# Small triangular systems kept with the row outermost: strides moved from two transposes to the products and copies around them

## What is computed

```python
def step(S, inp):                       # for every mode m and head h
    q_t, k_t, v_t, b_g, b_beta = inp
    S = S * jnp.exp(b_g)[..., None, None]
    kv = jnp.einsum('mbhk,mbhkv->mbhv', k_t, S)
    dv = (v_t[None] - kv) * b_beta[..., None]
    S = S + k_t[..., :, None] * dv[..., None, :]
    o_t = jnp.einsum('mbhk,mbhkv->mbhv', q_t, S)
    return (S, o_t)
_, ys = jax.lax.scan(step, S0, (qt, kt, vt, gt, bt))
```

## Time and profile before

| | us |
|---|---|
| median of 3 runs | 6816.04 |
| lowest, highest | 6806.51, 6821.66 |
| profiled execution | 6782.06 |
| its span, first to last instruction | 6780.4 |
| VectorE busy | 5129.9 |
| PE busy | 4499.9 |
| ScalarE busy | 3431.5 |
| POOL busy | 2767.9 |

### The profile page before, as it was taken

The page is one execution under the profiler, slowest core; times in us unless marked ns, Lnnn a source line. Parts: engine busy times, 40 slices in busy tenths (PEclk is TensorE's granted clock), DMA queues, the critical chain, the costliest instruction groups (busy, mean ns, idle before and its releaser), DMA issues. The chain is left out here.

```text
span 6780.4 us, 195918 instructions
## 1 busy us (share of the span) xinstructions
PE 4499.9 (66%) x78513; PEld 3871.6 (57%) x78513; DVE 5129.9 (76%) x9800; ACT 3431.5 (51%) x6010; POOL 2767.9 (41%) x1789
## 2 busy tenths in 40 slices
PE   1666666667666666666667666676666666655993
PEld 1556655556655656655566555566555665553662
DVE  4888888888888888888888888888888888881003
ACT  1555555555555555555555555555555555542220
POOL 3444343444343444443444444443434444433003
PEclk6788888888878888888888878788788888877996
DMA  2000000000000000000000000000000000013123
GB/s 91 2 6 6 6 5 6 6 5 3 5 5 5 6 6 6 6 5 6 5 5 3 5 5 6 5 6 6 5 6 5 6 3 5 5 35 110 61 69 108
DMA packets 77480, 109.71 MB, mean 16 GB/s; under 512 B 20577, under 2 KB 66209, under 8 KB 75425
## 3 DMA queue, kind: packets, MB, share of 16 engines
q1 hardware_dynamic: 67616, 71.42, 3.3%
q0 software_dynamic: 8960, 25.39, 1.2%
HBM read 57.89 MB, written 38.89 MB: 14 GB/s over the span
## 5 line engine op out<-in xcount | busy, mean ns | idle before, releaser
L1573 POOL TENSOR_TENSOR state<-state,gc_end 128x512 f32<-128x512 f32 x512 | 592.2, 1174 | 1626.7 <-PE bank L595 1586.2
L572 PE MATMUL bank<-state,ke 128*64 128x64 f32 x16384 | 641.4, 246 | 310.2 <-DVE outT L1309 169.4
L572 PEld LDWEIGHTS bank<-state,ke 128*64 128x64 f32 x16384 | 607.9, 159 | 379.8 <-issue 189.7
L608 PE MATMUL last_two<-dvs,kte 128*64 128x64 f32 x16384 | 691.8, 248 | 180.3 <-DVE dvs L1298 180.2
L589 PE MATMUL bank<-rhs,te 128*64 128x64 f32 x8192 | 408.0, 252 | 521.4 <-DVE rhs L1291 284.5
L847 ACT ACTIVATE ke<-kq 32x512 f32<-32x512 f32 x1024 | 643.0, 628 | 201.4 <-DVE kq L1223 187.7
L1272 DVE TENSOR_TENSOR last_two<-last_two,prod 128x31 f32<-128x31 f32 (+15 forms) x1984 | 693.0, 349 | 68.1
L608 PEld LDWEIGHTS last_two<-dvs,kte 128*64 128x64 f32 x16384 | 629.5, 161 | 196.6 <-DVE dvs L1298 187.3
L1270 DVE TENSOR_TENSOR prod<-bd,last_two 128x31 f32<-128x31 f32 (+15 forms) x1984 | 670.4, 338 | 68.3
L797 ACT ACTIVATE te<-tt 32x256 f32<-32x256 f32 x1024 | 421.9, 412 | 565.1 <-DVE tt L1275 554.5
L589 PEld LDWEIGHTS bank<-rhs,te 128*64 128x64 f32 x8192 | 341.1, 161 | 599.3 <-DVE rhs L1291 550.6
(11 more groups left out here) (257 smaller groups left out, 10393.1 us busy)
## 6 DMA issues: line engine op xcount, KB each, us to landing
w_sb<-in_L_ffn_W_dram SPq DMA_DIRECT2D x16, 1024.0 KB, 9.4
expert_rows<-ke SPq DMA_DIRECT2D x1, 8192.0 KB, 21.9
xrows<-expert_rows SPq DMA_DIRECT2D x16, 512.0 KB, 8.5
expert_outputs<-yrow POOLq DMA_DIRECT2D x16, 512.0 KB, 3.4
xt<-_attn_hidden_states_dram SPq DMA_DIRECT2D x32, 128.0 KB, 2.8
xr<-_attn_hidden_states_dram SPq DMA_DIRECT2D x32, 128.0 KB, 2.1
x_after_attention<-xr SPq DMA_DIRECT2D x32, 128.0 KB, 1.7
xo<-x_after_attention SPq DMA_DIRECT2D x32, 128.0 KB, 3.7
```

Of the source, the lines that this page charges most:

```text
L572: mm = pe.matmul(bank_mem[g][s, q % 4 * DK:q % 4 * DK + DK], ke[:, c, r, q, s], state[:, hh * HQ + q, r, :], start=(r == 0), stop=(r == 1))
L608: mm = pe.matmul(bank_upd[g][s, (q % 4) * P + r * DK:(q % 4) * P + r * DK + DK], kte[:, r, q, s], dvs[:, q, :], start=True, stop=True)
L1573: pool.tensor_tensor(sv, sv, gc_end[:, vh, 4 * g:4 * g + 4, c].unsqueeze(2).broadcast_to([P, 4, 2 * DK]), ALU.mult).then_inc(sem(f"state_f ...
```

## The change

`at` and `tt` are kept with the row outermost and chunk and group innermost. Both transposes then have contiguous patterns on both sides. The products of `chunk_systems` write `at` with a step of 32 floats, and the copies of `expand_te` read `tt` with a step of 32 floats. The number of instructions, their order and all semaphores stay the same.

```diff
-        tt = sb("tt", [P, NC, HQ, C])
+        tt = sb("tt", [P, C, NC, HQ])
...
-        at = cos_t[:].rearrange("p q t -> p (q t)").rearrange("p (c q i) -> p c q i", c=NC, q=HQ)
+        at = cos_t[:].rearrange("p q t -> p (q t)").rearrange("p (i c q) -> p i c q", i=C, c=NC)
...
-                    ins = act.activation(te[s, :, 32 * m:32 * m + 32], tt[s, c, :, :], ACT.Copy)
+                    ins = act.activation(te[s, :, 32 * m:32 * m + 32], tt[s, :, c, :].rearrange("p i q -> p q i"), ACT.Copy)
...
-                ln(dve.tensor_tensor(at[:, c], bv[:, :, 0, :], bd[:, :, c, :], ALU.mult))
+                ln(dve.tensor_tensor(at[:, :, c, :].rearrange("p i q -> p q i"), bv[:, :, 0, :], bd[:, :, c, :], ALU.mult))
...
-                ln(dve.transpose(a_prob, at.rearrange("p c q i -> p i (c q)")))
+                ln(dve.transpose(a_prob, at.rearrange("p i c q -> p i (c q)")))
...
-                vec(dve.transpose(tt[:].rearrange("p c q i -> p i (c q)"), t_prob), "tt_ready", u + 1)
+                vec(dve.transpose(tt[:].rearrange("p i c q -> p i (c q)"), t_prob), "tt_ready", u + 1)
```

## The result

The changed kernel takes 6762.07 us (median of 5 runs, 6757.04 to 6777.9) against 6806.51 us for the kernel before in the same series (5 runs, 6800.69 to 6821.66). The ratio is 0.9932, with a 95% interval of 0.9914 to 0.9951: 0.7% or about 44 us faster. The prediction was 6806 us, "no change that can be measured", with a range of 6766 to 6842.

What follows compares the result with a forecast made beforehand. The prediction took VectorE to bound the kernel, busy 76% of the span and 83% of the loop. Its terms, -47.6 - 41.5 + 41.5 + 37.8 = -9.8 us, gave 6806 us from the median 6816.04, range 6766 to 6842.

Steps and rivals of the forecast that it cites:

- the expansion: L797 on ScalarE: chunk 0's four stepped-read copies grow 1.28 us and delay PE in one half of each body, +37.8 us.
- nothing hides the products: L1256: VectorE's long wait for PE comes before the first product, so the stepped write costs its full +41.5 us.
- lines not edited keep their times: VectorE in the loop: the sum of -9.8 us has duration terms only for the edited lines.
- The range's far end: L1256: upper bound for the stepped write, 1.17 ns an element taken from L1217, which gives +77 us.
- the rival of a dear product: L1256: stepped write at 1.17 ns an element grows it by 77 us, net +26 us, 6842 us; chance 0.08.
- The cover: Half without the loop's turn: 0.1 us of chunk 0's 1.28 us longer expansion does not delay VectorE.
- The rival with ScalarE's read at VectorE's price: L797: four copies grow by only 0.74 us, 20.5 us in all, net -27 us, 6789 us; chance 0.25.
- The prediction's own sign: Check on all four edited lines: if they are as said but time moves over 20 us, the path claim is wrong.
- its claim about the path: In the loop, a microsecond taken from or given to VectorE moves the end by about that much, 64 times.
- late expansions: L797: possible cause if time moves over 20 us, ScalarE's expansions other than chunk 0's come late too.
- a swallowed gain: VectorE: possible cause if time moves over 20 us, its gain is lost in a wait further on.
- The one with the hidden write: L1256: products hide the stepped write, so the 41.5 us fall away, net -51 us, 6765 us; chance 0.08.

Runs made afterwards that it cites:

- the pair on one chip: Kernel before and changed kernel, both unchanged, run again on the same chip: 6808.28 us (ratio 1.0001) and 6758.26 us (ratio 0.9928).
- the split and the steps 21 and 25: Changed kernel with chunk 0's expansion copies in two parts, clip and scan moved to solve steps 21 and 25: 6731.6 us, ratio 0.9886 to before.
- the steps 19 and 24: Changed kernel with only the clip and scan moved, to steps 19 and 24 of the solve: 6741.22 us, ratio 0.990 to before.

## Why the prediction was wrong

In the loops of the two first profiles, 44.1 us apart, the prediction's -9.8 us becomes the measured difference by these steps: the wait behind the expansion -9.4 against the predicted size, the clip and the scan -15.7, three shorter waits of VectorE -17.9, the products +2.3, the two transposes +1.8, all else +4.5. Two of the prediction's steps failed outright, that nothing hides the products and that lines not edited keep their times; a third, the expansion, was sized too high.

**The four edited lines.** L1261 was said to lose 47.6 us and lost 47.6. L1275 was said to lose 41.5 and lost 41.1, so nothing of its step was PSUM's. The products were given +41.5, from the transpose's write, and took +44.6 (598 - 424 = 174 ns, 0.68 an element). The range's far end, 1.17 ns, and with it the rival of a dear product, fell. The Trainium skill (Vector Engine (DVE) Microarchitecture Reference, section 5.2) had given +43 by its hop row and +95 by its row of 24 words; the measured +44.6 sides with the first, and the second is not borne out for 32 floats.

**The expansion.** The mechanism was right: 33 waits of PE before and after, and the loss in one half of the body. Its size was off. A copy grew by 235 ns, not 320 (0.92 ns an element for 1.25). The price came from L893, a copy of 32 elements in 128 partitions, set against contiguous times that were worked out and not measured. By the copies of 128 and 256 above (1.82 ns an element, 185 ns fixed) a stepped copy of 32 would be 243 ns, an estimate; L893 takes 258, and why it takes more is not shown. The cover was 0 instead of 0.1 us: four copies grow by 0.94 us and 32 times that is 30; the idle time before L1298 grew by 29.8 (29.0 in the pair on one chip), predicted +37.8. That is 8 us of the error. The rival with ScalarE's read at VectorE's price lay 0.2 ns an element below. (The 591 ns that the prediction gives for its copy should be 599, 412 + 0.73 x 256.)

**"Nothing hides them."** This step, on the products of L1256, failed. The longest wait does come before the first product, as was said, but other waits of VectorE for PE stand behind the products and shrink when these take longer: inside the loop 5.3 us less before L1248 and 5.7 less before L1316. The runs with one layout each show that this goes with the products: with `at` alone the idle time before L1248 falls from 21.5 to 16.1 us and before L1316 from 40.5 to 34.8, with `tt` alone the two stay at 20.8 and 40.5. The wait before L1256 itself is 6.9 us shorter in the loop, but with `at` alone it is only 0.7 us shorter than in the first profile, and it varies between executions of the kernel before (88.0, 98.6 and 92.0 us of waiting for PE), so this part is not shown to be the products'. Together these are 17.9 us, of which 11 are shown.

**The missing term.** The other fault, of about the same size, is what the sum left out: it took for granted that only edited lines change in duration. The two short instructions inside the solve did too, by 15.7 us in the two first profiles, 17.6 in the loops of the pair on one chip, and 25 to 31 with `at` alone. The trace of before showed them in the same view as the earlier trace rows, a scan of 128 elements at 1719 ns, four times its least, and I did not ask why. The prediction's own sign pointed here: were the four lines as said and the time off by more than 20 us, its claim about the path would be wrong. It then named two causes, late expansions or a swallowed gain, and both would have made the kernel slower.

**What sets how long they are held** can be read a step further. From the start of L1261, medians over 31 bodies:

| | clip starts | L1564 starts | scan starts | last L1538 ends |
|---|---|---|---|---|
| before | 10.03 | 10.22 | 15.81 | 17.63 |
| after | 9.28 | 8.94 | 15.56 | 16.35 |

VectorE comes 0.75 us earlier to the clip, by the shorter transpose. But POOL's chain is earlier too, by 1.3 us, more than the transpose gives: L1564 waits for ScalarE's copy, which waits for PE. In the trace of before it starts at two places, around 10.3 or around 9.2. Which, goes with the granted clock in the 6 us around L1261's start. The view of stretches (after the length, five busy times, each with its count, then the clock) has for before, in the bodies with L1261 at 3257.06 and at 1217.69:

```profile
3252.06:3258.06 6.00, 5.10 (x71) 4.57 (x72) 5.43 (x9) 1.38 (x4) 1.02 (x1) 0.72 0.01 4
1212.69:1218.69 6.00, 5.09 (x78) 4.69 (x79) 5.43 (x9) 1.99 (x5) 1.01 (x1) 1.00 0.02 4
```

and for after, in the body with L1261 at 3055.64:

```profile
3050.64:3056.64 6.00, 5.45 (x80) 5.00 (x81) 5.43 (x9) 1.49 (x3) 1.02 (x1) 1.00 0.02 4
```

At 1.00 the whole stretch has the upper level, 2.4 GHz; at 0.72 part of it has the lower. In the first body PE's products at L544 take 4.73 us in the timeline of before:

```profile
3255.56 4.73 PE L544 MATMUL bank<-wv_sb,hT 128*128 128x256 f32 x16
```

and in that of after 3.72:

```profile
3053.20 3.72 PE L544 MATMUL bank<-wv_sb,hT 128*128 128x256 f32 x16
```

and all that hangs on it, down to L1564, comes later by about that. All 31 bodies of each trace fall in one of the two kinds, with no exception:

| | bodies at 0.72 | clip + scan there | bodies at 1.00 | clip + scan there |
|---|---|---|---|---|
| before | 20 | 2.50 us | 11 | 1.58 us |
| after | 5 | 0.72 | 26 | 1.85 |
| `at` alone | 13 | 0.72 | 18 | 1.82 |

The share is the kernel's own: three traces of before have 20, 22 and 20 bodies at 0.72, three of after 5, 6 and 5. From the rows: (20 x 2.50 + 11 x 1.58) less (5 x 0.72 + 26 x 1.85) is 67.4 - 51.7 = 15.7 us, the measured 15.7. Within one trace the holds account for the bodies' lengths as well: from L1261 to the next one a body at 0.72 is 0.91 us longer than one at 1.00 before, and 1.13 shorter after, where clip and scan differ by +0.92 and -1.13. Where nothing is held, with the split and the steps 21 and 25, the two kinds (16 and 15 bodies) differ by 0.10 us in the mean, 0.44 in the median. So the length goes mostly with the holds and not with the clock of that stretch itself, though with the steps 19 and 24 in after a body at 0.72 is 1.62 us longer and the holds explain only 0.92. That is an observation over the bodies, not an experiment: no run set the clock. Why the clock is granted so differently to the two kernels stays open. It also makes the expectations for the moved instructions too simple, since they took POOL's chain as fixed: in after with the two at steps 19 and 24, 26 of 31 bodies are at 0.72, where after has 5.

**The rivals and the base.** None of the rivals came true as told. The one with the hidden write gave 6765, near the result, but for a write that costs nothing, and it costs in full: had it come true, that would have been luck. The slower one with 1.17 ns an element took its price from L1217, whose extra time is a wait for POOL (1.08 us behind its end in all 64 cases) and no price of an access; the bound had no ground in that row. Last, the prediction set its sum against the profiled 6782.06 and carried it to the median. That was the right way: the profile of before had a tail of 735.4 us, while its median, 34 us higher, is like those of the series with tails of 760. Had I taken the two profiles' difference as the result, 20 us, it would have hidden half of the gain.

## What to carry to other kernels

When an edit shortens or lengthens one instruction of a busy engine, look, before you add up, for instructions of that engine whose mean is far above their least: they are held by something, and their price depends on when they start. Look for waits of that engine behind the edited instruction as well: they hide part of what it costs. Read the distribution of such a line, not its mean, and set its ends beside the ends of the engine that shares the ports. Such gains do not add: measure each step with the next one in place, and compare loops on one chip, not two single profiles.

## What the hardware showed that was not expected

- A clip (tensor_scalar, 64 x 128, 278 ns alone) and a scan with two SBUF inputs (416 ns alone) on VectorE take up to 2.43 and 2.48 us when a POOL instruction runs at their start, and end about 0.08 and 0.27 to 0.28 us after it. Six clips in three of the traces started 5 to 46 ns ahead of the POOL instruction and were held by it all the same. Operations of 1024 elements with two SBUF inputs (1225 ns alone) end 1.08 us after it; together they lose 178 us in this kernel. VectorE's transposes of 1024 elements stay at 1245 ns beside a running POOL.
- A step of 32 floats costs VectorE 0.73 ns an element in a transpose's read, 0.63 in its write and 0.68 in a product's write, and ScalarE 0.87 to 0.93 in a copy's read: 32 x 256 goes from 412 to 647 or 651 ns, 32 x 128 from 307 to 418.
- The same kernel has a tail of 734 to 736 us in one series and of 759 to 763 in others, with medians of 6784.74 and 6806 to 6807 us, while its loop agrees within 18 us (5841.3, 5858.6, 5847.2). Within a series the tail is the same for every version.
- The granted clock of one stretch comes in two values, 0.72 and 1.00, from body to body, and their share is steady for a kernel and differs between kernels that do the same work in the same order (20, 22, 20 bodies of 31 at 0.72 before; 5, 6, 5 after).
- The same 16 products of PE (L589) take 1.12 us behind 7.28 us without work, at a granted clock of 0.50, and 0.69 us behind 1.31 us without work, at 1.00.
